# Graph attention on one core: seven-product units for the score tiles, three to a pass from the sixth pass on

## The reference

```python
h = max(layernorm(x), 0)
q, k, v = h @ Wq.T + bq, key @ Wk.T + bk, value @ Wv.T + bv
s = (q @ k.T) / 64 * adj
s = where(abs(s) < 1e-5, -1e9, s)
out = x + (softmax(s, axis=-1) @ v) @ Wm.T + bm
```

## Time and profile before

| | |
|---|---|
| median of 3 runs | 1548.4 us |
| profiled execution | 1546.85 us |
| its span, first to last instruction | 1545.0 us |
| PE, DVE, ACT, POOL busy | 1522.7, 1061.2, 633.7, 217.9 us |
| TensorE clock granted | 1.000 of full speed |
| DMA, mean | 183 GB/s |

### The profile page before, as it was taken

The page is one execution under the profiler, slowest core; times in us unless marked ns, Lnnn a source line. Parts: engine busy times, 40 slices in busy tenths (PEclk is TensorE's granted clock), DMA queues, the critical chain, the costliest instruction groups (busy, mean ns, idle before and its releaser), DMA issues.

```text
span 1545.0 us, 23780 instructions
## 1 busy us (share of the span) xinstructions
PE 1522.7 (99%) x7064; PEld 700.5 (45%) x7064; DVE 1061.2 (69%) x2191; ACT 633.7 (41%) x1040; POOL 217.9 (14%) x291
## 2 busy tenths in 40 slices
PE   8998999999999999999999999999999999999998
PEld 5543444444444444444444444444444444444444
DVE  5989777766667666666766666676666767676662
ACT  5776433434343333334333334343333434333332
POOL 6164000020020101002010010201001020200100
PEclk9999999999999999999999999999999999999999
DMA  9834786678868687686868768676866868787664
GB/s 346 280 78 98 184 200 154 155 194 217 200 164 205 150 229 173 168 209 157 206 155 231 173 162 210 154 211 163 223 171 162 212 149 216 170 211 174 147 163 109
DMA packets 459508, 283.24 MB, mean 183 GB/s; under 512 B 377411, under 2 KB 385859, under 8 KB 459334
## 3 DMA queue, kind: packets, MB, share of 16 engines
q1 hardware_dynamic: 459456, 282.67, 72.7%
q10 hardware_dynamic: 6, 0.01, 0.0%
HBM read 175.38 MB, written 15.73 MB: 124 GB/s over the span
## 4 chain that ended last, share of the span: by engine, by line
PE 92%; DVE 3%; ACT 2%; DMA 2%; issue 1%; SPq 0%; ACTq 0%; DVEq 0%
PE R L833 15%; PE R L835 15%; PE R L834 15%; PE S L833 11%; PE S L835 11%; PE S L834 11%; PE M L833 3%; PE M L835 3%; PE M L834 3%; PE R L951 1%; PE R L904 1%; DMA pT<-ph 0%; DMA Kbuf<-key_factors 0%; DVE Vbuf L1581 0%; DMA pT<-osb 0%
## 5 line engine op out<-in xcount | busy, mean ns | idle before, releaser
L1293 ACT ACTIVATE drop<-Zbuf 128x512 f32<-128x512 f32 x256 | 161.1, 629 | 687.9 <-DVE cmx L1605 557.7
L833 PE MATMUL R<-Vbuf,pT 128*128 128x512 f16 x1008 | 382.1, 379 | 4.8 <-DMA pT<-ph 2.4
L835 PE MATMUL R<-Vbuf,pT 128*128 128x512 f16 x1008 | 382.0, 379 | 0.0
L834 PE MATMUL R<-Vbuf,pT 128*128 128x512 f16 x1008 | 382.0, 379 | 0.0
L833 PE MATMUL S<-Kbuf,qT 128*128 128x512 f16 x738 | 279.7, 379 | 0.0
L834 PE MATMUL S<-Kbuf,qT 128*128 128x512 f16 x738 | 279.7, 379 | 0.0
L835 PE MATMUL S<-Kbuf,qT 128*128 128x512 f16 x738 | 279.7, 379 | 0.0
L1657 DVE SCALAR_TENSOR_TENSOR Zbuf<-S,rs,adjb 128x512 f32<-128x512 f32 x178 | 133.5, 750 | 210.2 <-PE S L835 199.8
L1605 DVE CUSTOM_DVE_ANT_0 Zbuf<-drop,Zbuf 128x512 f32<-128x512 f32 x256 | 178.2, 696 | 0.0
L833 PEld LDWEIGHTS R<-Vbuf,pT 128*128 128x128 f16 x1008 | 98.6, 98 | 125.8 <-DMA pT<-ph 4.9
L835 PEld LDWEIGHTS R<-Vbuf,pT 128*128 128x128 f16 x1008 | 98.6, 98 | 118.9
(11 more groups left out here) (277 smaller groups left out, 1828.7 us busy)
## 6 DMA issues: line engine op xcount, KB each, us to landing
Kbuf<-key_factors SPq DMA_DIRECT2D x134, 512.0 KB, 4.2
adjb<-in_adj_dram SPq DMA_DIRECT2D x256, 256.0 KB, 2.9
xq<-in_x_dram SPq DMA_DIRECT2D x32, 256.0 KB, 2.8
Kbuf<-in_L_gnn_key_dram SPq DMA_DIRECT2D x8, 1024.0 KB, 13.7
xr<-in_x_dram SPq DMA_DIRECT2D x32, 256.0 KB, 3.0
out_dram<-xr SPq DMA_DIRECT2D x31, 256.0 KB, 4.3
Vbuf<-in_L_gnn_value_dram SPq DMA_DIRECT2D x7, 1024.0 KB, 7.9
key_factors<-early SPq DMA_DIRECT2D x32, 128.0 KB, 2.3
```

The lines of the kernel that those rows point to most:

```text
L833: nc.tensor.matmul(ps, lhs[0], rhs[0], start=start, stop=False, skip_group_check=added)
L834: nc.tensor.matmul(ps, lhs[0], rhs[1], start=False, stop=False, skip_group_check=added)
L835: return nc.tensor.matmul(ps, lhs[1], rhs[0], start=False, stop=stop, skip_group_check=added)
L1293: nc.scalar.activation(drop[:, :], tile_of(s.i, s.j), ACT.Abs).then_inc(abs_ready, 1)
```

## The change: a third unit, and another order

From pass 5 on there are three units to a pass, the third of groups (3, 2); passes 3 and 4 keep two. The even block's order is now plain, plain, unit 0 of the first, unit 0 of the second, unit 1 of the first, unit 0 of the third, unit 1 of the second, unit 1 of the third (groups 0, 1, 5, 7, 4, 3, 6, 2). In the odd block steps 8 to 12 and 14 are unit tiles. With two units, steps 5 and 7 are plain.

Product T2 and the addition of `W[0]` move from a unit's step 0 to its step 1, and product B21 moves from after the first quarter of the PV to after the third. So in a `unit == 1` step DVE makes both sums between the products T2, T1 and B22. The row mixes are made from step 0 on, and split in two halves, in ACT's step 2 (after its exponential) and in DVE's steps 2 and 3 (after `drop`). `SUM_U` and `SUM_W` lie in other slots of `Zbuf`, and the odd block's probabilities are taken in another order. Eight factors are kept (the four new ones in the space of groups 2 and 3), and 13 are loaded in a pass. Three of these wait for a unit's product T1 (`unit_mm`) and are issued after the probabilities' DMA. 24 pieces are made instead of 16, until step 66.

```diff
-        UNITS = [(5, 4), (7, 6)]
+        UNITS = [(5, 4), (7, 6), (3, 2)]
...
-        FIRST_ORDER, SECOND_ORDER = [0, 1, 2, 3, 5, 4, 7, 6], [4, 0, 5, 1, 6, 2, 7, 3]
-        SECOND_PROBS = [4, 5, 6, 7, 0, 1, 2, 3]
-        UNIT, NU, MAKE_STEP, FIRST = 4, len(UNITS), 19, 4
+        FIRST_ORDER, SECOND_ORDER = [0, 1, 5, 7, 4, 3, 6, 2], [4, 2, 5, 3, 6, 0, 7, 1]
+        FIRST_PROBS, SECOND_PROBS = [2, 3, 4, 5, 6, 7, 0, 1], [6, 7, 2, 3, 0, 1, 4, 5]
+        UNIT, NU, MAKE_STEP, FIRST = 4, len(UNITS), 19, 6
+        TWO_FROM, THREE_FROM = 3, 5
...
+        U_SLOTS, W_SLOTS = [6, 7, 3], [2, 0, 1]
+        SUM_U, SUM_W = [[z_slot(1, k) for k in slots] for slots in (U_SLOTS, W_SLOTS)]
+        FULLS = [z_slot(0, 4), z_slot(0, 6)]
+        mixes = Zbuf[:, 0, 2 * CW:4 * CW]
...
+        LATE = [W[0], S[0], S[1]]
...
(SP)
+            FACTOR_STEPS = {3: ((0, "B22"), 4), 4: ((1, "T1"), 5), 5: ((2, "B22"), 4), 8: ((0, "T4"), 4), 9: ((2, "T4"), 5),
+                            10: ((1, "T3"), 6), 11: ((1, "T4"), 4), 12: ((1, "B21"), 5), 13: ((0, "T1"), 6), 15: ((0, "B21"), 4)}
...
+                if s.strassen and s.j in FACTOR_STEPS:
+                    what, q = FACTOR_STEPS[s.j]
...
+                        wait(sp, scores_done, s.t)
+                        load_factor(what, q)
...
+                if s.three and s.j in (4, 7) or s.strassen and s.j == 6:
+                    w = (4, 6, 7).index(s.j)
+                    wait(sp, unit_mm, 2 * s.before + 2 * w + 2)
+                    load_factor(((2, "T1"), (0, "T3"), (2, "T3"))[w], (6, 5, 6)[w])
...
(PE)
                     elif s.unit == 0:
                         wait(pe, z1_ready, s.t - 1)
-                        unit_product(S[s.j % 2], qT[:, 0, :, 0:2, :], 2 * s.w, True).then_inc(unit_mm, 1)
...
-                        unit_product(W[0], qS[:, :, 2:4, :], 2 * s.w + 1, True).then_inc(unit_mm, 1)
+                        unit_product(S[s.j % 2], qT[:, 0, :, 0:2, :], factor_at(s, "B11")[0], True).then_inc(p1_mm, 1)
                     elif s.unit == 1:
                         wait(pe, z1_ready, s.t - 1)
+                        wait(pe, s_ready, 2 * s.nth + 1)
+                        unit_product(W[0], qS[:, :, 2:4, :], factor_at(s, "T2")[0], True).then_inc(unit_mm, 1)
+                        unit_product(S[s.j % 2], qS[:, :, 0:2, :], landed_factor(s, "T1"), True).then_inc(unit_mm, 1)
...
-                        if s.unit == 0 and m == 1:
+                        if s.unit == 0 and m == CM - 1:
+                            wait(pe, p1_ready, s.count + 1)
+                            unit_product(S[s.j % 2], qT[:, 0, :, 2:4, :], landed_factor(s, "B21"), False).then_inc(scores_done, 1)
                         if s.unit == 1 and m == CM - 1:
+                            wait(pe, mixed, 2 * s.count + 2)
+                            wait(pe, s_ready, 2 * s.nth + 2)
...
(ACT)
                 if s.unit == 0:
+                    wait(act, p1_mm, s.count + 1)
+                    wait(act, p_lo, PASS * (s.i - 1) + NC + SECOND_PROBS.index(U_SLOTS[s.w]) + 1)
                     nc.scalar.activation(SUM_U[s.w], S[s.j % 2][:, :], ACT.Copy).then_inc(p1_ready, 1)
...
                 if s.strassen and s.j == 2:
-                    nc.scalar.activation(qS[:, 0, :, :].rearrange("p s n -> p (s n)"), mixes, ACT.Copy).then_inc(s_hi, 1)
+                    for k in range(2):
+                        wait(act, s_made, 2 * s.nth + k + 1)
+                        nc.scalar.activation(qS[:, 0, 4 * k:4 * k + 4, :].rearrange("p s n -> p (s n)"), mixes[:, k * CW:(k + 1) * CW], ACT.Copy)\
+                            .then_inc(s_hi, 1)
...
(DVE)
-                if s.unit == 0:
-                    wait(dve, unit_mm, 6 * s.nth + 3 * s.w + 2)
-                    nc.vector.tensor_tensor(SUM_U[s.w], W[0][:, :], SUM_U[s.w], ALU.add).then_inc(mixed, 1)
                 if s.unit == 1:
+                    wait(dve, p1_ready, s.count + 1)
+                    wait(dve, unit_mm, 2 * s.count + 1)
+                    nc.vector.tensor_tensor(SUM_U[s.w], W[0][:, :], SUM_U[s.w], ALU.add).then_inc(mixed, 1)
+                    wait(dve, unit_mm, 2 * s.count + 2)
...
                     nc.vector.tensor_tensor(SUM_W[s.w], S[s.j % 2][:, :], SUM_U[s.w], ALU.add).then_inc(mixed, 1)
                     tile_max(s)
...
+                if s.strassen and s.j in (2, 3):
+                    low_of_mixes(s, s.j - 2)
```

More of the change, by code:

```diff
@@ L249, in z_slot @@
             return Zbuf[:, p, g * CW:(g + 1) * CW]
-        SUM_U, SUM_W = [z_slot(1, one) for one, _ in UNITS], [z_slot(1, two) for _, two in UNITS]
-        FULLS = [z_slot(0, 4), z_slot(0, 5)]
-        mixes = Zbuf[:, 0, (NC - 2) * CW:NC * CW]
+        U_SLOTS, W_SLOTS = [6, 7, 3], [2, 0, 1]
+        SUM_U, SUM_W = [[z_slot(1, k) for k in slots] for slots in (U_SLOTS, W_SLOTS)]
+        FULLS = [z_slot(0, 4), z_slot(0, 6)]
+        mixes = Zbuf[:, 0, 2 * CW:4 * CW]
         qS = ring_slot(MIX_Q).rearrange("p (h s n) -> p h s n", h=2, s=2 * ND)
-        XF = W[0]
+        XF = M0
+        LATE = [W[0], S[0], S[1]]
         CHAIN = {"T1": 3, "T2": 2, "T4": 2, "T3": 3}
@@ L420, in __init__, with factor_at @@
                 self.adj_n = (PASS // ADJ_SLOTS) * i + j // ADJ_SLOTS
+        def factor_at(s, what):
+            if s.three:
+                found = {**KEPT_TWO, **KEPT_THREE}.get((s.w, what))
+                turns, passes, loads = TURNS_THREE, s.i - THREE_FROM, {q: (THREE_FROM - TWO_FROM) * len(TURNS_TWO[q]) for q in RING_Q}
+            else:
+                found = KEPT_TWO.get((s.w, what))
+                turns, passes, loads = TURNS_TWO, s.nth, {q: 0 for q in RING_Q}
+            if found is not None:
+                return found, None
+            q = next(q for q in RING_Q if (s.w, what) in turns[q])
+            return q, 16 * (loads[q] + len(turns[q]) * passes + turns[q].index((s.w, what)) + 1)
         def by_pool(j):
@@ L548, in step @@
                     h_T(s)
[L549 to L566, removed]
+                if s.strassen and s.j in FACTOR_STEPS:
+                    what, q = FACTOR_STEPS[s.j]
+                    what = (1, "B22") if what == (2, "B22") and not s.three else what
+                    if (s.three or what[0] < 2) and (s.prefetch or s.j < 12):
+                        sp.wait_ge(kt_stored, 16 * (2 * len(PIECES) if s.three else 32))
+                        wait(sp, scores_done, s.t)
+                        load_factor(what, q)
                 if s.has_scores and s.more_adj:
@@ L617, in step @@
                 if s.making is not None:
-                    if s.making in (1, 3, 5, 7, 9, 11):
+                    if s.making in range(1, 2 * 3 * NU, 2):
                         w, k = divmod(s.making // 2, 3)
@@ L636, in step @@
                         sp.wait_ge(scores_done, 47)
[L637 to L643, removed]
+                    for what, q in ([((0, "B21"), 4), ((0, "T1"), 6)], [((1, "B21"), 5)])[s.t - 49]:
+                        load_factor(what, q)
+                if isinstance(s.t, int) and s.i == THREE_FROM - 1 and 10 <= s.j < 14:
+                    sp.wait_ge(kt_stored, 16 * 2 * len(PIECES))
+                    sp.wait_ge(kb_stored, 16 * 3 * NU)
+                    sp.wait_ge(scores_done, s.t)
+                    what = list(KEPT_THREE)[s.j - 10]
+                    load_factor(what, KEPT_THREE[what])
                 if s.c == 7 and s.has_out:
@@ L815, in step @@
                     rstd_of(s.stats)
-                if s.strassen and s.j == 1:
+                if s.strassen and s.j == 0:
                     row_mixes(s.i)
@@ L1000, in _, with landed_factor @@
             sum_over_partitions(wrow[:, :], sum_w).then_inc(aside_mm, 1)
+            def landed_factor(s, what):
+                q, loads = factor_at(s, what)
+                if loads is not None:
+                    wait(pe, kr_in[q], loads)
+                return q
             def unit_product(ps, lhs, q, start):
@@ L1596, in make_factor, with low_of_mixes @@
                                             XF[:, :] if second is None else second, op).then_inc(x_step, 1)
+            def low_of_mixes(s, k):
+                wait(dve, s_hi, 2 * s.nth + k + 1)
+                high, low = [qS[:, h, 4 * k:4 * k + 4, :].rearrange("p s n -> p (s n)") for h in range(2)]
+                nc.vector.tensor_tensor(low, mixes[:, k * CW:(k + 1) * CW], high, ALU.subtract).then_inc(s_ready, 1)
             def tile_max(s):
```

126 lines of the change are left out of this document (58 added, 68 removed).

## The result

The changed kernel took 1653.7 us (median of 4 runs, 1650.6 to 1655.2) against 1548.2 of the kernel before (4 runs, 1546.7 to 1549.1): a ratio of 1.068, interval 1.066 to 1.070. The prediction had the sign and placed the waits inside a pass; its time, 1611 us, was 43 us short, and the range ended 12 us too low. What it missed above all is the first pass with units.

The account below looks back on a forecast made before the run. PE's work alone was taken to set a pass's length. Waits of 68.2 (11 passes with three units) and 7.0 (two passes with two), plus 3 for the making, less 14.2 of matmuls: + 64 on 1546.85, 1611 us, range 1578 to 1642.

Parts of the forecast that it names:

- step 3: All 13 unit passes: PE waits 1.6 us for ACT's copy to SUM_U, queued behind the exponential and half copies of mixes.
- s3: The moment at which step 3's first product starts on PE; the prediction counts step 3's times from it.
- step 4: All 13 unit passes: PE's B22 waits 1.9 us for DVE's two additions, which follow the mixes' and row's low halves.
- s4: The moment at which step 4's first product starts on PE; the prediction counts step 4's times from it.
- Step 5: The 11 passes with three units: PE waits 0.6 us for ACT's copy for the third unit.
- Ring loads: Odd block, 11 passes: late-issued factor loads, landing in 4.2 us, make PE wait 1.2 us at step 9, 0.9 at 12.
- the rival that they keep up: Ring loads land in 3.4 us or earlier waits give the queue time: 11 x 1.6 us go, 1593 us; chance 25%.
- the rival that the DMA engines become the bound: Steps 8 to 11: one added 512 KB load costs some 1.9 us more a pass, 1632 us; chance 18%.
- The making of the factors: Eight more pieces made in steps 50 to 66, beside units and ring loads: 3 us in all, from nothing to 8.
- The sums are ready in time: Steps 3 and 4: PE runs through without waits, leaving only the 14.2 us gain, 1533 us; chance 6%.
- half of the waits: Steps 3 and 4 overlap more than the prediction can see, 1550 to 1580 us; chance 7%.
- the rival of the other side: Same rival as "The sums are ready in time"; it decides at 1.29 us of waits per pass, worth 6 matmuls.

Follow-up runs that it names:

- experiment 1: The changed kernel with ACT's exponential of steps 2 and 4 issued behind the next step's copy to SUM_U: 1634.8 us.
- experiment 2: The changed kernel with the mixes' second low half moved to DVE's step 2 and the row's low half behind step 4's two additions: 1625.5 us.
- experiment 3: The changed kernel with SP issuing the ring loads for steps 9 and 12 earlier, in steps 7 and 9 ahead of the probabilities' DMA: 1646.2 us.
- experiment 6: The changed kernel with the edits of experiment 1, experiment 2, experiment 3 and experiment 5 at once: 1582.4 us.
- experiment 10: The changed kernel with the edits of experiment 1, experiment 2 and experiment 5, the ring loads for steps 9 and 12 issued early on ACT's queue: 1583.1 us.
- experiment 11: The changed kernel with the edits of experiment 1, experiment 2 and experiment 5, without the ring loads for steps 9 and 12 (kept factors read instead): 1555.7 us.
- experiment 9: The changed kernel with the edits of experiment 1, experiment 2 and experiment 5, the ring loads of steps 11, 12 and 13 issued a step later: 1588.9 us.
- experiment 5: The changed kernel with units from pass 4 instead of 3, kept factors loaded in steps 59 to 62, first ring loads in 62 and 63: 1635.4 us.

## Why the prediction was right in direction and short in size

**Steps 3 and 4: right.** For step 3 the copy was to end 4.83 behind s3; it ended 4.98 behind (s3 = 850.97). The absolute value began 0.40 later than worked out, and from there to the copy's end took 0.25 less. For step 4 the two additions were to end at s4 + 6.40; they ended at s4 + 6.46 (s4 = 858.05). At the pace of matmuls the waits are 1.9 and 2.15 us where 1.6 and 1.9 were forecast. Experiments 1 and 2 took them away by the reordering alone, step 3's but for 0.5 us.

**Step 5: right**, 0.50 against 0.6.

**Ring loads: right in place and nearly in size, not in what holds them up.** Steps 9 and 12 wait 1.65 and 1.16 us (1.2 and 0.9 forecast). The loads landed in 4.3 us in the median. So the rival that they keep up fell, and the 3.2 us estimated from the Trainium skill's page (DMA: Bandwidth & Descriptors, section Anatomy of one DMA) were too short here, for 512 KB on SP's queue. But the prediction treated this wait as a matter of late issue, and the rival that the DMA engines become the bound as another case. Here they go together: early issue, on either queue, moves the wait to the probabilities (experiments 3, 6 and 10), and of the edits tried only leaving out the two loads removes it (experiment 11, 30.8 us, where 11 x 2.1 = 23.1 were forecast). Whether the bytes as such decide or the order in which the engines take them stays open; experiment 9, which moved loads from behind without a gain, speaks for what is under way before.

**The making of the factors and the start of the units: the term that failed.** It was taken as 3 us, "from nothing to 8", after the one pause of 1.6 us in the kernel before. Pass 3 lost 25.1 us. The 3.5 forecast for its steps 3 and 4 did not come there: PE's waits in its window name loads of factors, the row projection and once the probabilities (11.3, 5.6 and 0.4 us), not ACT's copy or DVE's addition.

The first part is a load that kept its place while its use moved. The change begins the first unit in step 50 of the program instead of step 52, but the last of the four kept factors is loaded in step 48 as before. SP's rows of that load, in the kernel before and in the changed one:

```profile
339.88 0.43 SPq L523 DMA_DIRECT2D Kbuf<-key_factors  x1
```

```profile
340.80 0.43 SPq L554 DMA_DIRECT2D Kbuf<-key_factors  x1
```

Before, it landed after 4.8 us, and the first unit's first product started at 349.25. Now PE had run out of work at 339.98, the load landed after 5.8 us, and PE, which counts all four kept loads before a unit's first product, stood:

```profile
346.74 0.58 PE L861 MATMUL S<-Kbuf,qT 128*128 128x512 f16 x1 [6.77 <-DMA Kbuf<-key_factors]
...
361.80 0.58 PE L861 MATMUL S<-Kbuf,qT 128*128 128x512 f16 x1 [4.52 <-DMA Kbuf<-key_factors]
```

The factor itself, T2 of the second unit, is used only in step 54; no run tries a wait for the needed ones alone. The second part is the second row: the second unit's B21 was issued at 357.56, when PE already stood, behind a store of the making. The prediction put its two more kept loads (the change has four) at nothing, "since they are ahead of need by a step", and of the first ring loads it said that they "come just in time too", without a price of their own. A load without slack ought to have been priced at its whole issue and landing.

The third part is the row projection, 4.6 us late: ACT stood 6.01 us behind a store of the making, and with it the row's split that SP was to transpose. This part is read from the trace; no run tests it alone.

```profile
433.73 0.38 ACT L1303 ACTIVATE early<-R 128x256 f16<-128x256 f32 x1 [6.01 <-DMA key_factors<-early]
```

The fourth part is the clock, 0.91 in the pass: behind the three long pauses 39 matmuls started mostly 0.43 us apart instead of 0.216, 7.9 us in all. The pauses inside the window come to 16.3 us, so the two hold 24.2 of the 25.1. With experiment 5, which begins the units a pass later, most of this goes (18.3 us in all).

**The gap of 44 us in the span** is then: pass 3, 18.6 beyond its 3.5 and the term of 3; the ten passes 5 to 14, 6.95 each against 6.2 - 1.29 = 4.91, so 20.4; pass 4, 1.8; the tail, 2.6; the start, 0.9. Of the 20.4, some 13 are waits that came out longer than forecast (7.5 a pass in the mean of the ten against 6.2, since not every pass has all six), and about 7 are the clock, below.

**The other rivals.** "The sums are ready in time" and "half of the waits" are out by PE's list of waits. What was right in the rival of the other side is its arithmetic: with the waits of steps 3 to 5 and the two loads gone, a pass takes 90.36 us (experiment 11), 0.3 less than before, since 0.7 of the 1.3 us that 6 matmuls are worth is still lost in step 3, and small waits on DMAs take some of the rest. That run still ends 7.6 us above the kernel before, most of it because its pass 4 begins at 438.0 us instead of 432.3 and takes 93.25.

## What to carry to other kernels

Ask of each op that PE will wait for what stands ahead of it on its engine in program order, and add it up from the moment at which that row is released: here it gave waits of 2 us to within 0.3, on engines that are idle for a third of the time and more. Where a pipeline starts, price every load that has no slack at its issue plus its landing, and every step that shares an engine with the start-up work; a small guess is no bound. When a change moves the first use of something, look up whether its load moves too. Before a late DMA is issued earlier, leave it out once: if that gains and the early issue does not, the moment of issue is not the limit; what is under way beside it has to be looked at.

## What the runs showed of the hardware

**The clock fell in or behind some single pauses of 2 us and more, and stayed down for some microseconds.** Before, the granted clock was 1.00 in all passes with units. Windows of the changed kernel, first around the pause of 6.77 us, then around a pause of step 4 in a later pass (columns as in the earlier trace rows, the clock third from the end):

```profile
342.00:346.00 4.00, 0.00 (x0) 0.00 (x0) 0.00 (x0) 0.00 (x0) 3.70 (x6) 0.74 1.41 303
346.00:350.00 4.00, 3.26 (x8) 1.17 (x9) 0.00 (x0) 0.50 (x2) 1.09 (x1) 0.50 0.80 281
764.00:768.00 4.00, 2.00 (x9) 0.63 (x7) 2.65 (x5) 0.80 (x2) 0.00 (x0) 0.89 0.57 165
768.00:772.00 4.00, 4.00 (x14) 1.55 (x13) 2.55 (x4) 1.17 (x2) 0.00 (x0) 0.68 0.00 1
```

0.50 is 1.2 GHz, and a matmul is then up to 0.63 us long in the rows instead of 0.38. In 764 to 772 the two windows' 0.89 and 0.68 are mixes of both levels. Four of the ten passes (7, 10, 12 and 13) had this after step 4's pause of 2.00 us, at some 1.7 us each. Five of the other six had the same pause and kept 1.00, so a pause of 2 us does not always bring it. With that pause gone (experiment 2) none of the ten passes had it; one such stretch is left there in pass 4 (0.60 from 496 to 500 us), behind a pause of 2.30 us for the row projection.

**A transposing DMA's issue on SP takes longer when more loads are under way.** The one of the row in step 9 took 1.23 us, 3.58 in experiment 3 with two ring loads ahead of it on SP, and 3.68 in experiment 10, where one of the two was on ACT's queue.
